# A graph network on one core: in both GAT passes a group's closing is divided into five steps, with a turn of the next group between each two

## The reference

```
def _gat_conv(x, src, dst, W, a_src, a_dst, b, heads, out_c, concat):
    xw = (x @ W).reshape(n, heads, out_c)
    e = leaky_relu(asrc[s] + adst[d], 0.2)          # one number per edge and head
    ex = exp(e - segment_max(e, d)[d])
    att = ex / (segment_sum(ex, d)[d] + 1e-16)
    return segment_sum(xw[s] * att, d) + b
x1 = elu(layer_norm(gat_conv(h, W1, 4 heads of 16)) * ln1_g + ln1_b)
z  = elu(layer_norm(gat_conv(x1, W2, 1 head of 64)) * ln2_g + ln2_b)
x  = x + z;   h = relu(layer_norm(x))               # what the GCN layer reads
```

## Time and profile before

| | us |
|---|---|
| median of 3 runs | 13329.96 |
| runs, least and most | 13327.62, 13337.75 |
| the profiled execution's own time | 13332.53 |
| its span in the trace | 13330.8 |
| pass 1 in the trace | about 4262 to 6324 |
| pass 2 in the trace | about 6471 to 8570 |

### The profile page before, as it was taken

How to read it: one execution, slowest core, us unless ns; L and a number is a source line. 1 busy time by engine, 2 the same in 40 slices (tenths; PEclk the granted TensorE clock), 3 DMA queues, 4 the chain that set the end, 5 groups by cost and what they waited for, 6 DMA issues and landing times. The chain is left out here.

```text
span 13330.8 us, 107772 instructions
## 1 busy us (share of the span) xinstructions
PE 2243.3 (17%) x7664; PEld 1456.1 (11%) x7664; DVE 6297.5 (47%) x21149; ACT 1706.1 (13%) x5627; POOL 8506.9 (64%) x8805
## 2 busy tenths in 40 slices
PE   8730000000000000000000000012222233333334
PEld 6620000000000000000000000001111112222223
DVE  9992333333344444444444444312222237777765
ACT  0000000000001000000011111000000014444443
POOL 0017466677656767776767777676666647777775
PEclk9755555555555555555555555555555555555555
DMA  0001233333311222222111111122222224444442
GB/s 10 0 14 39 28 27 27 26 29 28 27 21 29 32 33 33 33 33 31 26 25 27 27 27 27 26 49 47 47 47 48 48 52 107 108 107 107 107 101 64
DMA packets 1006418, 574.69 MB, mean 43 GB/s; under 512 B 757826, under 2 KB 855635, under 8 KB 1005953
## 3 DMA queue, kind: packets, MB, share of 16 engines
q0 software_dynamic: 307520, 409.04, 18.8%
q1 hardware_dynamic: 587723, 101.69, 4.7%
q10 hardware_dynamic: 111088, 63.12, 1.6%
HBM read 485.71 MB, written 87.37 MB: 43 GB/s over the span
## 5 line engine op out<-in xcount | busy, mean ns | idle before, releaser
L973 POOL DMA_INDIRECT got<-gat_tab,list x3280 | 3113.8, 949 | 1323.4 <-issue 970.7
L973 POOL DMA_INDIRECT got<-rel_tab,list x1640 | 1648.0, 1005 | 709.3 <-issue 448.4
L973 POOL DMA_INDIRECT got<-gcn_tab,list x1640 | 1548.5, 944 | 740.6 <-issue 495.7
L973 POOL DMA_INDIRECT got<-h_tab,list x1640 | 1567.9, 956 | 676.1 <-issue 492.4
L1709 DVE TENSOR_REDUCE chunk_sum<-got 128x64 f32<-128x256 f32 (+1 forms) x436 | 239.7, 550 | 1577.2 <-DMA got<-gcn_tab,list 1492.7
L1059 DVE TENSOR_TENSOR prod<-got,h 128x256 f32<-128x256 f32 (+1 forms) x436 | 179.6, 412 | 1309.2 <-DMA got<-h_tab,list 1203.5
L1641 PE MATMUL p_t<-ident,hg 128*128 128x128 f32 x98 | 24.6, 429 | 4436.6 <-DVEq L1546 4436.6
L1446 DVE COPY e<-top 128x4 f32 (+1 forms) x872 | 189.3, 217 | 1224.1 <-DMA got<-gat_tab,list 966.6
L535 POOL DMA_INDIRECT info_tab<-info,rank_i x98 | 125.4, 1279 | 977.1 <-DVEq L512 947.5
L2204 PE MATMUL p_gate<-got,ident 128*128 128x256 f32 (+1 forms) x872 | 510.3, 689 | 1382.8 <-DVE gate L2041 1382.8
L1588 ACT ACTIVATE p<-e 128x20 f32<-128x20 f32 (+3 forms) x872 | 185.4, 213 | 3719.1 <-DVE e L1465 3536.9
(11 more groups left out here) (436 smaller groups left out, 8709.3 us busy)
## 6 DMA issues: line engine op xcount, KB each, us to landing
own<-own_tab SPq DMA_DIRECT2D x436, 160.5 KB, 2.4
got<-gat_tab,list POOLq DMA_INDIRECT x3280
rel_tab<-rows ACTq DMA_DIRECT2D x98, 386.0 KB, 2.9
got<-h_tab,list POOLq DMA_INDIRECT x1640
got<-gcn_tab,list POOLq DMA_INDIRECT x1640
got<-rel_tab,list POOLq DMA_INDIRECT x1640
own_tab<-own ACTq DMA_DIRECT2D x98, 160.5 KB, 3.4
chunks_src<-rows_src SPq DMA_DIRECT2D x480, 4.5 KB
```

What stands on the lines that cost most here:

```text
L973: pool.indirect_dma_start(r.got[:, q, j, :], None, table, at(r.lists[s][:, c, j:j + 1]))\
```

## The change

`close(g)` is taken apart into `divide`, `scale`, `elu` and `renorm`; with `finish` these are five steps. Between each two of them stands a turn of the next group, written out, on VectorE; ScalarE's parts (`deviation`, `both_sides`, `turned_rows`, `store`) are spread over the same turns. What is left of the group's turns runs in the loop as before. The operations themselves, their shapes and their number are the same; each step newly clears the chain's semaphore and counts a tick, the last group's closing stands behind the loop in one piece, and nothing changes on GpSimd, SP and PE. The number of turns in a group (9, 10, 12, 14, 14, 17, 20) always exceeds the five written out.

```diff
+            def divide(g):
                 blocks = bass.ds(g * GROUP, GROUP)
                 dve.sem_clear(close_step)
                 ch = Chain(dve, close_step)
...
                 tsc(st[:, 1, :], st[:, 0, :], 1.0 / D, LN_EPS, ALU.mult, ALU.add).then_inc(var_ready, 1)
+
+            def scale(g):
+                dve.sem_clear(close_step)
+                ch = Chain(dve, close_step)
                 dve.wait_ge(std_ready, g * NORMS + 1)
+                dve.sem_inc(r.tick, 1)
...
                 tt(Y[:, :, :], Y[:, :, :], vec(after.shift), ALU.add).then_inc(y_ready, 1)
+
+            def elu(g):
...
                 dve.wait_ge(ex_ready, g + 1)
+                dve.sem_inc(r.tick, 1)
...
-                    relu_norm(nc, dve, ch, xb, hg[:, :, :], sq[:, :, :], st, full, var_ready, std_ready,
-                              g * NORMS + 2)
-                dve.sem_inc(h_ready, 1)
+                    norm_variance(nc, ch, xb, hg[:, :, :], sq[:, :, :], st, full, var_ready)
+
+            def renorm(g):
+                if after.x is not None:
...
+                    dve.wait_ge(std_ready, g * NORMS + 2)
+                    dve.sem_inc(r.tick, 1)
+                    norm_scale(nc, ch, hg[:, :, :], sq[:, :, :], st, full)
+                    dve.sem_inc(h_ready, 1)
...
-            dve.sem_inc(stored, 16)
-            group(0)
-            close(0)
-            with dve.Fori(1, TURNS) as g:
-                group(g)
-                finish(g - 1)
-                close(g)
+            with dve.Fori(t0, t1) as i:
+                turn(i)
+            with dve.Fori(1, TURNS) as g:
                 t0, t1 = group_turns(dve, lists, g)
+                divide(g - 1)
+                turn(t0)
+                scale(g - 1)
+                turn(t0 + 1)
+                elu(g - 1)
+                turn(t0 + 2)
+                renorm(g - 1)
+                turn(t0 + 3)
+                turn(t0 + 4)
+                finish(g - 1)
                 one_block(nc, dve)
-                with dve.Fori(t0, t1) as i:
+                with dve.Fori(t0 + 5, t1) as i:
                     turn(i)
+            divide(TURNS - 1)
+            scale(TURNS - 1)
+            elu(TURNS - 1)
+            renorm(TURNS - 1)
             finish(TURNS - 1)
...
         @block.scalar
+                with act.Fori(1, TURNS) as g:
                     t0, t1 = group_turns(act, lists, g)
+                    deviation(g - 1, 1)
+                    turn(t0)
+                    both_sides(g - 1)
+                    turn(t0 + 1)
+                    if NORMS == 2:
+                        deviation(g - 1, 2)
+                    turn(t0 + 2)
+                    turn(t0 + 3)
+                    turned_rows(g - 1)
+                    turn(t0 + 4)
+                    store(g - 1)
+                    with act.Fori(t0 + 5, t1) as i:
                         turn(i)
```

More of the change, by code:

```diff
@@ L398, with norm_variance @@
 KEYS_OUT, KEYS_END = keys_out()
-def relu_norm(nc, dve, ch, x, h, sq, st, shape, var_ready, std_ready, n):
-    wide = lambda j: bc(st[:, j, :].unsqueeze(2), shape)
+def norm_variance(nc, ch, x, h, sq, st, shape, var_ready):
     ch.link(nc.vector.tensor_reduce(st[:, 0, :], x, AX, ALU.add))
     ch.link(nc.vector.tensor_scalar(st[:, 3, :], st[:, 0, :], 1.0 / D, None, ALU.mult))
-    ch.link(nc.vector.tensor_tensor(h, x, wide(3), ALU.subtract))
+    ch.link(nc.vector.tensor_tensor(h, x, bc(st[:, 3, :].unsqueeze(2), shape), ALU.subtract))
     ch.link(nc.vector.tensor_tensor(sq, h, h, ALU.mult))
@@ L410, in relu_norm, with norm_scale @@
     nc.vector.tensor_scalar(st[:, 1, :], st[:, 0, :], 1.0 / D, LN_EPS, ALU.mult, ALU.add).then_inc(var_ready, 1)
-    dve.wait_ge(std_ready, n)
+def norm_scale(nc, ch, h, sq, st, shape):
     ch.link(nc.vector.reciprocal(st[:, 3, :], st[:, 2, :]))
     ch.link(nc.vector.tensor_scalar(sq, h, 0.0, None, ALU.max))
-    ch.link(nc.vector.tensor_tensor(h, sq, wide(3), ALU.mult))
+    ch.link(nc.vector.tensor_tensor(h, sq, bc(st[:, 3, :].unsqueeze(2), shape), ALU.mult))
+def relu_norm(nc, dve, ch, x, h, sq, st, shape, var_ready, std_ready, n):
+    norm_variance(nc, ch, x, h, sq, st, shape, var_ready)
+    dve.wait_ge(std_ready, n)
+    norm_scale(nc, ch, h, sq, st, shape)
 def rank_nodes(nc, k, a):
@@ L1507, in turn @@
                 dve.wait_ge(e_ready, i * RING + RING)
-            def close(g):
+            tt, tsc = nc.vector.tensor_tensor, nc.vector.tensor_scalar
+            flat = lambda t: t.rearrange("p b d -> p (b d)")
+            wide = lambda j: bc(st[:, j, :].unsqueeze(2), full)
+            vec = lambda t: bc(t[:, :].unsqueeze(1), full)
+            def divide(g):
                 blocks = bass.ds(g * GROUP, GROUP)
@@ L1513, in close @@
                 ch = Chain(dve, close_step)
-                tt, tsc = nc.vector.tensor_tensor, nc.vector.tensor_scalar
-                flat = lambda t: t.rearrange("p b d -> p (b d)")
                 cols = state[:, blocks, 0:HW].rearrange("p b (h c) -> p b h c", h=heads)
-                wide = lambda j: bc(st[:, j, :].unsqueeze(2), full)
-                vec = lambda t: bc(t[:, :].unsqueeze(1), full)
                 ch.link(tsc(den[:, 0, :, :], cols[:, :, :, c], SM_EPS, None, ALU.add))
@@ L1534, in close @@
                 tt(Y[:, :, :], Y[:, :, :], vec(after.shift), ALU.add).then_inc(y_ready, 1)
+            def elu(g):
+                blocks = bass.ds(g * GROUP, GROUP)
+                dve.sem_clear(close_step)
+                ch = Chain(dve, close_step)
                 dve.wait_ge(ex_ready, g + 1)
+                dve.sem_inc(r.tick, 1)
                 ch.link(nc.vector.scalar_tensor_tensor(out=flat(Y[:, :, :]), in0=flat(ex[:, :, :]), scalar=1.0,
@@ L1564, in _ @@
                 return
-            def group(g):
-                t0, t1 = group_turns(dve, lists, g)
+            dve.sem_inc(stored, 16)
+            t0, t1 = group_turns(dve, lists, 0)
+            one_block(nc, dve)
+            with dve.Fori(t0, t1) as i:
+                turn(i)
+            with dve.Fori(1, TURNS) as g:
+                t0, t1 = group_turns(dve, lists, g)
+                divide(g - 1)
[8 more added lines that the diff above has]
+                finish(g - 1)
                 one_block(nc, dve)
-                with dve.Fori(t0, t1) as i:
+                with dve.Fori(t0 + 5, t1) as i:
                     turn(i)
-            dve.sem_inc(stored, 16)
-            group(0)
-            close(0)
-            with dve.Fori(1, TURNS) as g:
-                group(g)
-                finish(g - 1)
-                close(g)
+            divide(TURNS - 1)
+            scale(TURNS - 1)
+            elu(TURNS - 1)
+            renorm(TURNS - 1)
             finish(TURNS - 1)
@@ L1592, in turn, with deviation, both_sides, turned_rows @@
                                   .rearrange("a p c -> p a c"), again[:, :, :]).then_inc(again_out, 16)
-            def close(g):
-                act.wait_ge(var_ready, g * NORMS + 1)
+            def deviation(g, norm):
+                act.wait_ge(var_ready, g * NORMS + norm)
+                act.sem_inc(r.tick, 1)
                 nc.scalar.activation(st[:, 2, :], st[:, 1, :], ACT.Sqrt).then_inc(std_ready, 1)
+            def both_sides(g):
                 act.wait_ge(y_ready, g + 1)
+                act.sem_inc(r.tick, 1)
                 nc.scalar.activation(sq[:, :, :], Y[:, :, :], ACT.Relu)
                 nc.scalar.activation(ex[:, :, :], Y[:, :, :], ACT.Exp).then_inc(ex_ready, 1)
-                if NORMS == 2:
-                    act.wait_ge(var_ready, g * NORMS + 2)
-                    nc.scalar.activation(st[:, 2, :], st[:, 1, :], ACT.Sqrt).then_inc(std_ready, 1)
+            def turned_rows(g):
                 act.wait_ge(turned, g + 1)
+                act.sem_inc(r.tick, 1)
                 nc.scalar.activation(hT[:, :, :], p_t[:, :, :], ACT.Copy).then_inc(hT_ready, 1)
@@ L1617, in _ @@
             else:
-                def group(g):
+                t0, t1 = group_turns(act, lists, 0)
+                with act.Fori(t0, t1) as i:
+                    turn(i)
+                with act.Fori(1, TURNS) as g:
                     t0, t1 = group_turns(act, lists, g)
-                    with act.Fori(t0, t1) as i:
-                        turn(i)
[L1623 to L1628, removed]
+                    deviation(g - 1, 1)
[10 more added lines that the diff above has]
+                    with act.Fori(t0 + 5, t1) as i:
+                        turn(i)
+                deviation(TURNS - 1, 1)
+                both_sides(TURNS - 1)
+                if NORMS == 2:
+                    deviation(TURNS - 1, 2)
+                turned_rows(TURNS - 1)
                 store(TURNS - 1)
```

3 lines of the change are left out of this document (added).

## The result

The changed kernel takes 13169.44 us (median of 4 runs, 13165.01 to 13171.46) beside 13328.79 us for the kernel before in the same session; the ratio is 0.9879 [0.9862, 0.9896]. The forecast was 13165. The profiled execution took 13168.54 us, its span is 13166.8.

What follows compares the result with a forecast made beforehand. GpSimd's gathers set the pace, with time lost in list waits at closings. 13332.5 - 207.2 + 22.8 + 21 + 7 - 8.4 = 13167.7, less 2.6 for the median: 13165 us, range 13122 to 13203.

Steps and rivals of the forecast that it cites:

- what is to be had (207 us): GpSimd's list waits at six closings of each pass, beyond the ordinary 0.30 us: 85.6 + 121.6 us to give back.
- the overrun of `divide`: `divide` with the road to GpSimd's restart exceeds the ring's slack by 2.6 us (pass 1) and 1.2 (pass 2): 22.8 us stay.
- the jump back, 2.1 us: VectorE's enlarged loop over groups reloads 8 KB of code ahead of `divide`: five jumps per pass, 21 us in all.
- the slack: How long GpSimd still has work after VectorE's last sum of a turn: 15.8 us in pass 1, 16.3 in pass 2.
- The other steps, at nothing: `scale`, `elu` and `finish` with turn head and list fit behind written-out turns: 0 us, bounds 0 to 4.
- More gathers under wide operations, 7 us: About 4 and 9 newly covered gathers per closing, each 0.09 us slower, six times: 7 us lost.
- The ends of the passes, 8.4 us: `finish` no longer behind the last turn (3.3 and 2.9 us), no store wait in pass 1 (2.2): 8.4 us gained.
- One sign: In the changed profile, GpSimd's list waits at the first six closings fall from 15 and 21 us to under 5.
- the margins close (13121): Better rival: code stays or is fetched in time (13144), and `divide` no longer overruns either: 13121 us; chance 0.2.
- The worse case: Rival: each jump costs two loads, 4.2 us, and `elu` in pass 2 overruns by 0.7: 13190 us; chance 0.15.
- The waits did not move: Answers a rival: VectorE does not catch up between steps, so GpSimd waits at the next turns: 13330 us; chance 0.03.
- the gathers did not all pay 0.8 us: Answers a rival: wide VectorE operations slow all 228 covered gathers by 0.8 us, 182 us lost: 13340 us; chance 0.02.

Runs made afterwards that it cites:

- The large loop alone: Kernel before, closing in one piece, with five turns of each group written out in VectorE's loop over groups: 13349.14 us, ratio 1.002.
- one-split kernel: Changed kernel with `scale`, `elu` and `renorm` in one piece behind the first turn: 13203.38 us, ratio 0.9908 to the kernel before.
- the kernel with both: Changed kernel with VectorE's loop over groups written out and `divide` cut in two with a turn between: 13130.3 us, ratio 0.9849 to the kernel before.

## Why the prediction was right, point by point

**Where GpSimd idles, and what is to be had (207 us): right.** All six closings of each pass read alone give 85.2 and 121.5 us over the 0.30; three of six had been filled in from their neighbours.

**What is left there: the sum right, the shares not.** The forecast had 22.8 us for the overrun of `divide` and 21 for the jumps, 43.8; measured are 43.4, of which about 10.7 are the overrun and 32.7 the jumps (the first closing's wait taken for the overrun at all six of a pass). But the step "the jump back, 2.1 us" was mis-sized: it is 3.5 us in pass 1 in VectorE's timeline (5.54 against 2.01) and 2.9 in pass 2 (4.88 against 2.00). The 8 KB load from which the 2.1 came was the right kind of row and too small a price: two packets start in the idle time ahead of the step, and not one. The large loop alone showed 2.1 to 2.5 us of GpSimd's time at most closings, with the jump at another place. In exchange the overrun of `divide` is smaller. At the first closing of pass 1 it is 2.08 - 0.30 = 1.8 us, where the forecast had 2.6, and in pass 2 nothing, where it had 1.2. The step's own 8.0 us came out (4454.05 to 4462.10). What was too long is the road around it: the 4.95 and 5.73 us between closing and turn had been charged whole, beside 0.4 ahead of the step; divided between the two places they are 2.0 and 2.25 in pass 1. The whole road is 16.9 us instead of 18.4, and the slack 15.1 (4452.04 to 4467.13) instead of 15.8. Two errors cancelled, and that the sum came out is luck.

The rule of the Trainium skill that spoke against the change ("Runtime: NRT & Kernel Launch", "Instruction fetch mechanics") is borne out: loops of 585 and 505 instructions are fetched again at each jump, as the code packets in the idle time and its 36.6 us show, and straight code is not waited for.

**The other steps, at nothing: right.** With five steps no list wait stands behind `scale` or `elu`; the bound of 4 us for the latter was not needed. The one-split kernel shows what the cover is worth: 35 us in pass 2.

**More gathers under wide operations, 7 us: measured 10.6.** The gathers' sum grew by 6.3 and 4.3 us. The mean of 0.09 for each covered gather was an average over a price that depends on the moment: nothing for most, up to 0.88 for one.

**The ends of the passes, 8.4 us: too much.** From a pass's last gather to the next stage's first it is 45.5 instead of 49.7 us behind pass 1 and 50.6 instead of 51.7 behind pass 2, 5.3 together. In pass 1 `finish` now waits for PE and no longer for a store, as foreseen. The rest of the difference is a term that the forecast did not have. ScalarE around the square roots of the last closing of pass 2, before and now:

```profile
8528.00 1.28 ACT L1596 ACT_TABLE_LOAD   x1
8540.52 0.21 ACT L1596 ACTIVATE st<-st 128x14 f32<-128x14 f32 x1 [11.24 <-DVE st L1529]
```

```profile
8382.35 1.28 ACT L1639 ACT_TABLE_LOAD   x1 [9.65 <-DVE st L1538]
8383.64 0.21 ACT L1639 ACTIVATE st<-st 128x14 f32<-128x14 f32 x1
```

Before, ScalarE loaded the table of the square root while it waited for the variance; now the load stands behind the wait, and VectorE waits 1.76 us for each root instead of 0.3. In the other closings a turn hides that; the last has none. So in pass 2 `divide` begins 3.1 us earlier after the last gather, two roots cost 1.5 us each, and PE begins no earlier (32.98 us behind the last gather, 33.00 before). In pass 1 one root costs 1.5 of the 5.5 us forecast. The 1.1 us of pass 2 come up only at the landing of the next stage's list.

**The passes:** forecast to become 63 and 102 us shorter; with their ends, 54.9 and 103.4. Of the 164 us between the two profiled executions the passes are 158. The relational stage, which moves from run to run by as much, gave 8 and the first stage took back 2. The medians, 159.4 us apart, say the same as the passes. So the forecast of 164.8 was about 5 to 7 us too high, from pass 1: the jump there is dearer than its smaller overrun gives back, and end and gathers each take some more. One sign was missed: at four of the five closings behind a jump in pass 1 the list wait did not fall under 5 us, but to 5.77 to 5.85.

**The rivals.** That the margins close (13121) came true only once the jump was out of the way: 13130. The worse case was wrong in its place, the `elu`, and with 4.2 us somewhat nearer to the price of a jump than the 2.1 of the sum. The waits did not move, and the gathers did not all pay 0.8 us, though some do.

## What to carry to other kernels

Where a long piece of work on one engine starves another through a ring, cut it where each piece with one turn's head fits into the ring's slack; the slack and the piece can both be read from one closing in two timelines, and cuts beyond that (pass 1 here) bring nothing. A loop that such cutting makes long may pay at every jump back: put the jump at a place with slack or write the loop out, each of which was worth about another 0.2% here. And once no wait is left, the pacing engine's own instructions are the time; then what VectorE does at the moment of their issue begins to count.

## What was unexpected in the hardware

A gather that GpSimd issues while VectorE is in an operation with two f32 inputs in SBUF takes the rest of that operation plus 0.82 us, whatever its width (128x260 to 128x896): 1.82 us with 1.00 to go, 1.52 with 0.70, 1.42 with 0.60, 1.16 with 0.34, to within 0.01, in the kernel with both. The traces of all ten kernels agree. Of the gathers issued with at least 0.2 us of such an operation (of over 0.4 us) to go, 563 follow that sum to within 0.01 us; the other 131 were issued in its first 0.044 us and took the ordinary 0.94 or 0.95. Under a reduction, or under the sum of `finish` that reads one of its inputs from PSUM and writes 128x938 (0.63 us to go), a gather takes the ordinary 0.94. So a gather is either not touched or waits to the end of that operation; the mean of 0.95 hides it.

Two inputs are not the only case. An operation that has one input and passes 896 columns in 0.63 us instead of 1.09 (L414, in pass 2) met two gathers, both in the kernel with one split, and held them: 1.02 and 1.03 us with 0.20 and 0.21 to go.

The Trainium skill ("SBUF — State Buffer", "SBUF: two separate sides") describes a port pair of SBUF that whichever of VectorE and GpSimd begins first holds for a whole instruction, VectorE when its operation has two inputs in SBUF (against GpSimd work that reads SBUF) or runs in a fast mode with two ports. The runs agree with that for the gathers. They don't show it the other way round: of 922 operations of 128x896 with two inputs that VectorE began while a gather ran, none took over 1.12 us instead of 1.09. What in the last 0.82 us of a gather's 0.94 waits for VectorE no run shows.

The other surprise is the size of a jump back, 2.9 us in a loop of 505 instructions and 3.5 in one of 585, while straight code of several times that length runs without a stop that GpSimd would feel.
